# Best-32 attention: GpSimd marks what lies below in the upper half of the keys; exact path without its first search and last comparison

## What is computed

```python
scores = jnp.einsum('bthd,bghd->bhtg', Q, K) / np.sqrt(DH)
topv, topi = jax.lax.top_k(scores, K_TOP)            # K_TOP = 32
probs = jax.nn.softmax(topv, axis=-1)
attn = jnp.zeros_like(scores).at[bi, hi, ti, topi].set(probs)
attn_mean = attn.mean(axis=1)
V = x_vision @ Wv
c_t = jnp.einsum('btg,bgd->btd', attn_mean, V)
```

## Time and profile before

| | us |
|---|---|
| median of three executions (1164.32 to 1171.87) | 1168.22 |
| the profiled execution, its own time | 1164.9 |
| its span, first to last instruction | 1163.7 |
| VectorE busy, whole span | 829.5 (71%) |
| ScalarE busy | 627.7 (54%) |
| TensorE busy | 969.7 (83%) |
| GpSimd busy | 258.4 (22%) |
| the touched part, from about 718 to 1005 in the span | 287 |

### The profile page before, as it was taken

One profiled execution on the slowest core, in us unless ns is written; L12 is line 12 of the kernel. 1 busy time (PEld: TensorE's weight loads), 2 busy tenths in 40 slices (PEclk: granted clock), 3 DMA queues, 4 the chain that ended last, 5 costly groups with the idle time before them and its releaser, 6 DMA issues. The chain is left out here.

```text
span 1163.7 us, 20413 instructions
## 1 busy us (share of the span) xinstructions
PE 969.7 (83%) x7503; PEld 589.6 (51%) x7520; DVE 829.5 (71%) x1753; ACT 627.7 (54%) x1018; POOL 258.4 (22%) x281
## 2 busy tenths in 40 slices
PE   6997769999999999985879998518878878996586
PEld 5886624444444444443765565314455555744354
DVE  5775688999999999913542447998888786256447
ACT  3443317887887888872331114139999998202121
POOL 1000188899300000000000002003554632000010
PEclk9999959999999999997769998558799998997797
DMA  5867632223223223102011216302164226740000
GB/s 179 312 226 256 254 113 73 74 79 83 73 77 86 73 75 86 44 1 57 1 55 62 85 44 181 96 0 60 38 173 133 69 80 213 176 137 1 0 1 19
DMA packets 99319, 111.80 MB, mean 96 GB/s; under 512 B 26658, under 2 KB 75730, under 8 KB 99218
## 3 DMA queue, kind: packets, MB, share of 16 engines
q1 hardware_dynamic: 96802, 109.50, 31.2%
q10 hardware_dynamic: 2416, 0.99, 0.4%
HBM read 80.95 MB, written 29.43 MB: 95 GB/s over the span
## 5 line engine op out<-in xcount | busy, mean ns | idle before, releaser
L835 ACT ACTIVATE pT<-bank 128x512 f32<-128x512 f32 x512 | 278.4, 597 | 93.5 <-PE bank L752 72.2
L857 DVE TENSOR_REDUCE rmax<-bank 128x2 f32<-128x1024 f32 x256 | 307.3, 1223 | 26.5 <-PE bank L720 25.7
L764 PE MATMUL bank<-pT,V 128*17 128x256 f32 x2048 | 161.1, 387 | 4.7 <-ACT oT L841 4.6
L1600 PE MATMUL bank<-K1s,qs 97*128 97x512 f32 x256 | 116.1, 555 | 58.6 <-ACT below L1709 37.2
L752 PEld LDWEIGHTS bank<-qs,ks 49*128 49x128 f32 x1024 | 77.8, 187 | 112.4 <-ACT pT L835 98.9
L752 PE MATMUL bank<-qs,ks 49*128 49x256 f32 x1024 | 130.0, 332 | 2.3 <-ACT pT L835 0.5
L1864 POOL TENSOR_TENSOR total<-total,work 128x1024 f32<-128x1024 f32 x40 | 94.9, 2380 | 154.7 <-ACT work L1718 153.9
L720 PE MATMUL bank<-ks,qs 49*128 49x512 f32 x512 | 110.6, 427 | 16.4 <-DMA ks<-k_parts_d 9.2
L1600 PEld LDWEIGHTS bank<-K1s,qs 97*128 97x128 f32 x256 | 54.0, 224 | 73.9 <-ACT below L1709 38.6
L1770 DVE MAX8 cand<-work 128x8 f32<-128x128 f32 x384 | 76.5, 280 | 0.0
L764 PEld LDWEIGHTS bank<-pT,V 128*17 128x17 f32 x2048 | 34.6, 95 | 63.0 <-ACT pT L835 43.6
(11 more groups left out here) (442 smaller groups left out, 1789.5 us busy)
## 6 DMA issues: line engine op xcount, KB each, us to landing
k_parts_d<-kparts SPq DMA_DIRECT2D x48, 512.0 KB, 3.6
ks<-k_parts_d SPq DMA_DIRECT2D x381, 64.0 KB, 2.2
K1s<-k_parts_d SPq DMA_DIRECT2D x96, 128.0 KB
cn<-in_ctx SPq DMA_DIRECT2D x32, 384.0 KB, 3.6
cx<-in_ctx SPq DMA_DIRECT2D x16, 384.0 KB
w<-in_L_ffn_w SPq DMA_DIRECT2D x32, 128.0 KB
w2e<-in_L_ffn_w SPq DMA_DIRECT2D x16, 128.0 KB
W<-in_L_xattn_W SPq DMA_DIRECT2D x2, 1024.0 KB, 9.6
```

The costliest lines, as they stand in the source:

```text
L764: t = pe.matmul(bank[32 * c:32 * c + VW, 7, a * S:(a + 1) * S], V[:, b * NCH + 4 * g + c, h, :], pT[:, (at + 2 * (c // 2) + a) % 8, c % 2 ...
L835: p_made.up(act.activation(pT[:, at % 8, :], bank[:, 4 + at % 3, :], ACT.Exp))
L857: max_read.up(dve.tensor_reduce(rmax[p % 2][:, :, qt, c], bank[:, b0:b0 + 2, :], AX.X, ALU.max))
L1600: m = pe.matmul(bank[:, b0 + c, :], qs1[0:NROW1, b * H1 + h, q], K1s[h][0:NROW1, keys], start=True, stop=(what == "new"))
```

## The change

- `mark_below` on ScalarE stays for pieces 0 and 1 only. GpSimd marks pieces 2 and 3 of every tile, one instruction a piece: `score * steep < steep_thr`, which writes 1 or 0 into `below`. Its program becomes, per step `s`, the four adds of tile `s-2` and then the two marks of tile `s-1`.
- `minus` gets a second half, -STEEP times the identity, which TensorE uses for pieces 2 and 3. The number of matmuls is the same.
- The factor of the comparison now lies in SBUF (`steep`, a pair per tile: one for ScalarE, one for GpSimd), since the exact path needs another. On the usual path VectorE copies the pair from `usual` (a new instruction, 128x2 f32, in front of the one that writes `steep_thr`).
- On the exact path the first search over 4096 keys goes (the 8 best are the same as those of the candidates), and so does the last comparison; the marks read `LOW` against `FAR` instead. Three memsets of one column stand where one stood.
- `settle` waits for the marks of both engines.

```diff
-    minus = sb("minus", [P, P], BF16)
+    minus = sb("minus", [P, 2, P], BF16)
+    steep, usual = sb("steep", [P, 2, 2]), sb("usual", [P, 2])
...
-                pe.wait_ge(*below_made.at(4 * t + k + 1))
+                pe.wait_ge(*(below_made if k < 2 else marked).at(2 * t + k % 2 + 1))
...
-                    m = pe.matmul(bank[:, b0 + c, :], minus[:, :], below[:, keys], start=False, stop=True)
+                    m = pe.matmul(bank[:, b0 + c, :], minus[:, k // 2, :], below[:, keys], start=False, stop=True)
...
-                                         scale=-STEEP), n)
+                                         scale=steep[:, t % 2, 0:1]), n)
...
                 if 1 <= s < NTL:
-                    if k % 2:
-                        mark_below(s - 1, k - 1, 2)
                     if k == 1:
+                        mark_below(s - 1, 0, 2)
                         sum_best(s - 1)
...
                 if s == NTL:
-                    mark_below(s - 1, k, 1)
+                    if k < 2:
+                        mark_below(s - 1, k, 1)
...
-                dve.wait_ge(*below_made.at(4 * (t - 1)))
+                dve.wait_ge(*below_made.at(2 * (t - 1)))
+                dve.wait_ge(*marked.at(2 * (t - 1)))
             dve.reg_load(flagged, over_i[j][0:1, 0:1])
             with dve.If_ne(flagged, 0):
-                for k in range(KTOP // 8):
+                exact.up(dve.match_replace(home(t)[:, :], top[j][:, 0:8], home(t)[:, :], LOW))
+                for k in range(1, KTOP // 8):
                     take8(top[j][:, 8 * k:8 * k + 8], home(t)[:, :], home(t)[:, :], exact)
-                dve.wait_ge(*exact.at(NEX * t + 8))
-                exact.up(dve.tensor_scalar(home(t)[:, :], home(t)[:, :], LOW, -1e18, ALU.not_equal, ALU.mult))
-                exact.up(dve.memset(steep_thr[:, j:j + 1], 0.0))
+                exact.up(dve.memset(steep[:, j, 0:1], 1.0))
+                exact.up(dve.memset(steep[:, j, 1:2], -1.0))
+                exact.up(dve.memset(steep_thr[:, j:j + 1], FAR))
             with dve.If_eq(flagged, 0):
+                dve.tensor_copy(steep[:, j, :], usual[:, :])
                 dve.tensor_scalar(steep_thr[:, j:j + 1], top[j][:, KTOP - 1:KTOP], STEEP, None, ALU.mult).then_inc(exact.sem, NEX)
...
-        minus_made.up(dve.tensor_scalar(minus[:, :], identb[:, :], -1.0, None, ALU.mult))
+        for k, by in enumerate((-1.0, -STEEP)):
+            minus_made.up(dve.tensor_scalar(minus[:, k, :], identb[:, :], by, None, ALU.mult))
+            vec.do(dve.memset(usual[:, k:k + 1], (2 * k - 1) * STEEP))
...
+        def mark(t, k):
+            part = slice(k * 1024, (k + 1) * 1024)
+            pool.wait_ge(*picked.at(t + 1))
+            if t:
+                pool.wait_ge(*s_made.at(nth["cut", t - 1, k] + 1))
+            marked.up(pool.tensor_scalar(below[:, part], home(t)[:, part], steep[:, t % 2, 1:2], steep_thr[:, t % 2:t % 2 + 1],
+                                         ALU.mult, ALU.is_lt))
+
+        for s in range(1, NTL + 1):
+            if 2 <= s < LATE + 2 and (s - 2) % H1:
+                add(s - 2)
+            for k in (2, 3):
+                mark(s - 1, k)
```

More of the change, by code:

```diff
@@ L1453, in build @@
     NCN = 4
-    LOW = -3e38
+    LOW, FAR = -3e38, 1e30
     STEEP = 2.0 ** 66
     below = sb("below", [P, S2], BF16)
-    minus = sb("minus", [P, P], BF16)
+    minus = sb("minus", [P, 2, P], BF16)
     cand = sb("cand", [P, NG, 8])
@@ L1481, in build @@
         "s_made", "s_taken", "sel", "over_made", "over_summed", "over_in", "exact", "picked"))
-    lsum_made, ebias_made, added, below_made, e_summed = (flag(n) for n in (
-        "lsum_made", "ebias_made", "added", "below_made", "e_summed"))
+    lsum_made, ebias_made, added, below_made, marked, e_summed = (flag(n) for n in (
+        "lsum_made", "ebias_made", "added", "below_made", "marked", "e_summed"))
     late_added = flag("late_added")
@@ L1645, in best_tensor @@
             piece("new", 0, k)
-        pe.wait_ge(*minus_made.at(1))
+        pe.wait_ge(*minus_made.at(2))
         for g in range(4 * (NTL + 1)):
@@ L1854, in best_pool, with add @@
     def best_pool():
-        for t in range(LATE):
-            if t % H1 == 0:
-                continue
+        def add(t):
             acc = total[t // H1 % 3]
```

## The result

The changed kernel takes 1192.93 us, the median of four executions (1191.24 to 1196.79), beside 1170.05 us (1164.32 to 1172.73) for the kernel before in the same comparison. The ratio is 1.021, with a 95% interval of 1.0176 to 1.0244: slower by 2.1%, and 33 us above my 1160, outside the range. The profiled execution spans 1190.6 us from its first to its last instruction, 26.9 more than before.

What follows compares the result with a forecast made beforehand. VectorE's and ScalarE's loops were taken to run nearly level, plus one exact path where all wait. Terms -6.6, -11.4, -1.3, -1.95, +1.5 and +12 sum to -7.8 us: 1160 us by the median, range 1146 to 1177.

Steps and rivals of the forecast that it cites:

- exact path: In the one `settle` taking it, first search (4.56 us) and last comparison (2.24) go, two memsets come: -6.6 us.
- ScalarE's mark, last cast, last step: ScalarE's second mark leaves its loop, -11.4 us; last cast waits less, -1.3; TensorE's last quads start earlier, -1.95.
- the copy, its own time and its wait: VectorE's copy of the pair in 15 settles: +1.5 us own time, +12 waiting for GpSimd's adds.
- GpSimd's mark: GpSimd's two marks per step, taken at 1.2 us each, fit beside four adds (11.8 us against 12.2): no cost.
- Rival C: GpSimd's mark far slower, 3.3 us a piece, making GpSimd the bound in nine steps: 1168 us or more; chance 0.04.
- half an add, 1.2 us, is a fair mean, ten add steps: VectorE's copy in `settle` falls into a running GpSimd add and waits half of it in ten steps: +12 us.
- Rival B: GpSimd keeps VectorE's copy out until its row of ready instructions ends: +28 us of waiting, 1176 us; chance 0.20.
- 3 and more across two POOL instructions: Copy durations in us in the trace that would show GpSimd keeping VectorE out until its ready row ends.
- Nearly all of them go: VectorE's 12.9 us of waits before casting the sum of `over` nearly vanish; 1.5 left for TensorE: -11.4 us.
- rival D: TensorE takes ScalarE's place, so ScalarE's loop isn't shortened; later still at half clock: about 1168 us; chance 0.06.
- slower by more: Chance that the kernel comes out above 1180 us, beyond the 1% a measurement can tell: 0.13.
- The last step: TensorE's 2.24 us wait for the last mark goes; its last quads start 3.25 us earlier, 1.95 counted here.

Runs made afterwards that it cites:

- cheap marks: Changed kernel with GpSimd's comparison replaced by multiply by zero and add of zero: 1151.99 us (0.9857) with memsets for the copy, 1182.2 us (1.014) with the two-column copy.
- the kernel with the exact path alone: Kernel before plus the new exact path, factor in SBUF and two-column copy, ScalarE making all marks: 1185.04 us, ratio 1.0148.
- the marks first: Changed kernel with GpSimd's two marks of a step in front of the four adds instead of behind them: 1200.64 us, ratio 1.0311.

## Why the prediction was wrong

By its own steps, measured values from the ratios above:

| step | predicted | measured |
|---|---|---|
| exact path | -6.6 | -9 (-13 to -5) |
| ScalarE's mark, last cast, last step | -14.65 | -8 at a mark of 1.2 us |
| the copy, its own time and its wait | +13.5 | +33 beside cheap marks, +26 by itself, +5 (not clear of noise) in the change |
| GpSimd's mark | 0 | +36 without the copy, +8 with it |
| sum | -7.8 | +24.5 (1.021) |

In the order exact path, cheap marks, copy, true price, the four are -9, -8, +33 and +8, which makes +24. Copy and mark overlap, since a delay of the one falls into waits that the other has made; either of them alone would have made the kernel slower (1.0148 without GpSimd's marks, 1.0165 without the copy).

- **The step that failed: "I take 1.2, since it has one tensor input".** The mark takes 3.77 us. Both bounds were of other operations: a multiply and add below, an addition of two tensors above, and I took the number of inputs for what sets the price. It is the pair of operations that sets it, and with it GpSimd, whose 11.8 us of work a step "just fits" in the prediction, has 16.9 and becomes the bound. Rival C had the mechanism ("becomes the bound", a price of 3.3 us, "1168 or more") and 0.04 of the chance, on the ground that nothing in the trace spoke for it; nothing spoke against it either.
- **The second that failed: "half an add, 1.2 us, is a fair mean, ten add steps".** That the copy of two columns waits was right. Two things were wrong with its price. The first is where it stands. I worked its place out from ScalarE's second mark, when the rows had it directly: the cast of 879.16 puts the copy at 879.97, and the second of the two adds that start at 877.48 starts at 879.88. So in six steps with quads a whole add is ahead of it, not half of one: its fifteen instances last 18.2 us in the kernel with the exact path alone, where I had 13.5. The second is what such a wait costs. I took it one for one; it stands in front of ScalarE's mark, and TensorE then comes later too: 26 us for 18.2, and 2.9 a step (16.85 against 13.94) for a copy of 2.3.
- **Rival B**, that GpSimd keeps VectorE out until its row of ready instructions ends, is neither the rule nor out. Against it: in the changed kernel the copy at 983.01 ended at 983.49, while the second add of its row ran on to 985.80. For it: by the sign that I had named, "3 and more across two POOL instructions", two copies beside cheap marks (3.19 and 3.59 us) and the one of 9.51 with the marks first waited to the end of the row. No run shows what decides between the two. In the changed kernel itself no copy waited through more than one instruction. That B's +28 us lies near the measured +26 and +33 is luck in the main, since most of the long copies waited for a single add.
- **The exact path** was right in the trace to 0.1 us.
- **"Nearly all of them go"**, of VectorE's waits for the sum of `over`: with cheap marks they are still 12.8 us in nine in 780 to 1000, where they were 15.0 in twelve, though the kernel is faster. This term, too, was sized too large. The profiles speak for a part of rival D, TensorE in ScalarE's place, and for the condition that it named: "at its half clock in a step it would be late by more". It isn't shown, as said above.
- **The chances** hold a slip: a third of B and part of C make 0.11 at most for "slower by more", not 0.13.
- **The last step** turned round. TensorE waits for GpSimd's last mark where it was to wait no more:

```profile
1004.60 0.51 PE L1601 MATMUL bank<-K1s,qs 97*128 97x512 f32 x1 [1.60 <-POOL below L1876]
...
1010.17 0.79 PE L1601 MATMUL bank<-K1s,qs 97*128 97x512 f32 x1 [4.36 <-POOL below L1876]
...
1012.08 1.06 PE L1625 MATMUL bank<-ident,total 128*128 128x128 f32 x4
```

The last quads start 1012.08 - 992.52 = 19.6 us behind the last cast, against 986.45 - 970.76 = 15.7 before: 4 us more, in place of 2 less.

## What to carry to other kernels

A price bounded by rows of other operations isn't bounded: before moving work to an engine, find a row of the very pair of operations, or measure it, and leave a chance for an engine that turns out three times slower wherever it would have no slack. Where two engines keep each other out, the price hangs on the moment at which they meet. Where one engine's work releases both, that moment is much the same in each step, and it can be read from the trace before the change: look at the instruction that stands there already, rather than taking half of the other's. And look for the form that avoids it: two memsets of one column, at 0.06 us each, did the work of the copy in the change, and where one factor was enough, a copy of one column took 0.15.

## What the runs showed of the hardware

- GpSimd's two-operation instruction on 128x1024 takes 1.05 us for multiply and add, 3.65 to 3.78 for multiply and less-than, 3.71 for subtract and minimum; 2.85 for one comparison or one subtraction alone.
- A VectorE copy of one column took 0.15 us in 15 of 15 cases, ten of which started within a GpSimd add. A copy of two columns that started within an add ended 0.02 or 0.03 us behind an add in every run here: as a rule behind the add that ran, but with cheap marks twice behind the next (3.19 and 3.59 us), and with the marks first too (2.65 and 4.25 us). One that started at the end of a mark there waited for the four adds behind it, 9.51 us. A memset of one column took 0.06 us, within adds and marks too.
- GpSimd's mark kept the copy out in two parts of its time only. In the changed kernel ten copies started within a mark. Five of them started up to 0.8 us into it and ended 1.20 to 1.22 us into it, such as the one of 822.32, which ended at 823.45, in the mark that started at 822.23 and ran for 3.79 us. Three started 1.25 to 1.95 us into it and took 0.17. One started 2.62 us into it and was kept until it ended (888.08, 1.20 us); with the marks first one that started 3.47 us into a mark was kept to its end too. One doesn't fit: the last copy, at 993.34, started 0.09 us into a mark and took 0.18.
- VectorE's additions of two tensors and the marks also slowed each other. Of the four marks at the end three take 3.78 us, and the additions that begin 0.3 to 0.4 us behind their starts take 1.82 to 1.98 us instead of 1.23. The fourth, beside which three additions run at 1.21 to 1.23 us and one at 1.81, takes 5.59. No run was made to test it.
